# Query preparation for the next block moved from the end of an attention block to its head boundaries

## The reference

```python
xn = x / jnp.maximum(l2, 1e-12) * scale_norm * gamma
qkv = jnp.einsum('bnc,fc->bnf', xn, w_qkv)
q = q * scale_attn
sim = jnp.einsum('bihd,bjhd->bhij', q, k)
sim = jnp.where(causal_mask, neg, sim)
attn = jax.nn.softmax(sim, axis=-1)
out = jnp.einsum('bhij,bjhd->bihd', attn, v)
return jnp.einsum('bnf,cf->bnc', out, w_out)

x = x + _layernorm(_L0_attn_ref(_layernorm(x, axis=-1), ...), axis=-1)
x = x + _layernorm(_L0_ffn_ref(_layernorm(x, axis=-1), ...), axis=-1)
```

## Time and profile before

| what | us |
|---|---|
| time, median of 2 runs (7944.98 and 7990.62) | 7967.8 |
| profiled execution, its own time | 7980.3 |
| its span, slowest core (core 2) | 7978.8 |
| spans of the 8 cores | 7902.2 to 7978.8 |
| TensorE busy, share of the span | 4850.2, 61% |
| ScalarE busy | 3005.3, 38% |
| VectorE busy | 2903.3, 36% |
| GpSimd busy | 481.4, 6% |

### The profile page before, as it was taken

How to read it: one execution, slowest core, us unless ns; L and a number is a source line. 1 busy time by engine, 2 the same in 40 slices (tenths; PEclk the granted TensorE clock), 3 DMA queues, 4 the chain that set the end, 5 groups by cost and what they waited for, 6 DMA issues and landing times.

```text
span 7978.8 us, 56275 instructions; the slowest of 8 cores (7902.2 to 7978.8 us)
## 1 busy us (share of the span) xinstructions
PE 4850.2 (61%) x18281; PEld 1766.1 (22%) x18624; DVE 2903.3 (36%) x4937; ACT 3005.3 (38%) x4569; POOL 481.4 (6%) x612
## 2 busy tenths in 40 slices
PE   3545666877875233366566676887814767766553
PEld 1221222222221111122122222222202222222211
DVE  4444333122123666444333322222124333334445
ACT  1212444564563121122234554464612333333332
POOL 0000100000000000000000000000021011010000
PEclk8776888988987666566688888798956778878776
DMA  2111111001001122200211101001043011010111
GB/s 76 36 64 45 48 41 41 24 27 37 22 24 49 60 90 77 95 32 27 71 48 43 42 27 39 22 27 36 12 128 104 0 37 48 3 44 25 42 43 61
DMA packets 120312, 362.13 MB, mean 45 GB/s; under 512 B 24464, under 2 KB 24464, under 8 KB 120016
## 3 DMA queue, kind: packets, MB, share of 16 engines
q1 hardware_dynamic: 120016, 358.51, 13.5%
HBM read 291.07 MB, written 67.37 MB: 45 GB/s over the span
## 4 chain that ended last, share of the span: by engine, by line
PE 51%; DVE 22%; DMA 12%; ACT 8%; issue 3%; POOL 2%; SPq 1%; DVEq 0%; ACTq 0%
PE pf L1119 9%; PE pf L805 8%; PE pf L845 8%; PE pf L834 7%; ACT probs L815 4%; PE pf L638 3%; PE pf L898 3%; PE pf L664 3%; DMA xq<-xbuf 3%; PE pf L739 3%; PE pb L481 2%; DMA xbuf<-xq 2%; POOL probs L823 2%; DVE xq L571 2%; PE pf L1123 2%
## 5 line engine op out<-in xcount | busy, mean ns | idle before, releaser
L815 ACT ACTIVATE probs<-pf,negM_col 128x512 bf16<-128x512 f32 x2304 | 1585.4, 688 | 819.7 <-PE pf L805 764.4
L834 PE MATMUL pf<-probs,v_sb 128*128 128x512 bf16 x2286 | 908.9, 398 | 461.5 <-ACT probs L815 267.1
L481 PE MATMUL pb<-ident_bf,prep_bf 128*128 128x128 bf16 x1536 | 198.6, 311 | 1356.9 <-DVE prep_bf L337 461.0
L856 DVE RECIPROCAL rcp_row<-pf 1x512 f32<-1x512 f32 x128 | 428.3, 3346 | 1449.1 <-PE pf L845 1445.3
L845 PE MATMUL pf<-probs,ones_col 128*1 128x512 bf16 x2304 | 893.8, 388 | 8.1 <-ACT probs L815 3.7
L805 PE MATMUL pf<-qT,kT 128*128 128x512 bf16 x2178 | 855.4, 401 | 4.0 <-issue 4.0
L823 POOL TENSOR_SCALAR_AFFINE_SELECT probs<-probs 128x512 bf16<-128x512 bf16 x512 | 314.4, 614 | 5457.1 <-ACT probs L815 5457.1
L1131 ACT ACTIVATE ySB<-pf,bcol 128x512 bf16<-128x512 f32 x384 | 264.0, 687 | 730.7 <-PE pf L1123 727.2
L540 ACT ACTIVATE sq<-pb 128x1024 bf16<-128x1024 bf16 x128 | 131.1, 1024 | 907.0 <-DVE cols L534 907.0
L481 PEld LDWEIGHTS pb<-ident_bf,prep_bf 128*128 128x128 bf16 x1536 | 148.0, 141 | 1412.5 <-DVE prep_bf L337 422.2
L1119 PE MATMUL pf<-hT,wbuf 128*128 128x512 bf16 x1497 | 402.9, 414 | 48.7 <-ACT ySB L1131 41.7
(11 more groups left out here) (134 smaller groups left out, 5531.9 us busy)
## 6 DMA issues: line engine op xcount, KB each, us to landing
xq<-xbuf SPq DMA_DIRECT2D x128, 512.0 KB, 3.2
xbuf<-xq SPq DMA_DIRECT2D x96, 512.0 KB, 2.6
xq<-x SPq DMA_DIRECT2D x64, 512.0 KB, 3.5
rcp_bc<-rowrt SPq DMA_DIRECT2D x128, 256.0 KB, 3.1
xq4f<-xbuf SPq DMA_DIRECT2D x64, 512.0 KB, 4.0
wstage<-wqkvT SPq DMA_DIRECT2D x48, 512.0 KB, 4.4
wstage_i<-qwT SPq DMA_DIRECT2D x48, 512.0 KB, 3.7
screp<-scT SPq DMA_DIRECT2D x384, 64.0 KB, 2.3
```

Source lines behind the costliest of these rows:

```text
L481: v = p.add("tensor", lambda e, j=j: e.transpose(M.pb[pslot][:, j, :], M.prep_bf[:, prep_slot, j * 128:(j + 1) * 128], M.ident_bf[:]), wai ...
L815: ev = p.add("scalar", lambda e, kc=kc, h=h, ps=ps: e.activation(M.probs[:, kc % 2, :], ps[:], AF.Exp, bias=M.negM_col[:, h:h + 1], scale= ...
L834: p.add("tensor", lambda e, h=h, kc=kc, pO=pO: e.matmul(pO[:], M.v_sb[:, kc, h * 128:(h + 1) * 128], M.probs[:, kc % 2, :], start=(kc == 0 ...
L856: rc = p.add("vector", lambda e, pR=pR: e.reciprocal(M.rcp_row[:], pR[0:1, :]), waits=rw, inc="ve")
```

## The change

The four tiles of `q_prep` are written one by one behind heads 0, 1, 2 and 3 of the block before, each behind that head's normalisation. Nothing is written behind head 4. The groups of `q_mm` for heads 0, 1 and 2 are written behind heads 5, 6 and 7. The other five groups stay behind the output projection. The last block (qt = 7) has no next block and is as before, and so is the preparation of block 0 ahead of the loop. No operation is added or removed.

```diff
-    def q_prep(qt):
-        evs = []
-        for tt in range(4):
+    def q_prep_tile(qt, tt, evs):
+        for tt in (tt,):
...
+    def q_prep(qt):
+        evs = []
+        for tt in range(4):
+            q_prep_tile(qt, tt, evs)
         return ("ve", max(evs))
+
+    def q_mm_group(fo, xnT_ready):
+        pfk = M.pf[fo % 2]
...
+        return qev
...
             p.pO_gate[hp] = ("ve", nv)
+            if qt + 1 < nq:
+                if h == 0:
+                    qp_evs = []
+                if h < 4:
+                    q_prep_tile(qt + 1, h, qp_evs)
+                    if h == 3:
+                        xnT_ready = ("ve", max(qp_evs))
+                else:
+                    qev_n = q_mm_group(h - 5, xnT_ready) if h >= 5 else None
+        attnout_ready = ("ve", p.c("ve"))
         p.feat8_gate = None
-        attnout_ready = ("ve", p.c("ve"))
-
-        if qt + 1 < nq:
-            xnT_ready = q_prep(qt + 1)
...
         if qt + 1 < nq:
-            qT_ready = q_mm(qt + 1, xnT_ready)
+            for fo in range(3, H):
+                qev_n = q_mm_group(fo, xnT_ready)
+            p.xnT_free[0] = p.add("scalar", _nop, inc="nf0")
+            qT_ready = ("ae", qev_n)
             negM_evs = bound_prep(qt + 1, qT_ready)
```

More of the change, by code:

```diff
@@ L729, in q_prep @@
             evs.append(emit_prep_to_xnT(p, M, tt, 0, tp))
+    def q_prep(qt):
+        evs = []
+        for tt in range(4):
+            q_prep_tile(qt, tt, evs)
         return ("ve", max(evs))
+    def q_mm_group(fo, xnT_ready):
+        pfk = M.pf[fo % 2]
+        w0 = [xnT_ready, wq_ready]
+        if p.pf_gate[fo % 2]:
+            w0.append(p.pf_gate[fo % 2])
+        for fi in range(NF):
+            mv = p.add("tensor", lambda e, fo=fo, fi=fi, pfk=pfk: e.matmul(
+                pfk[:], M.wbuf1[:, fi, fo * 128:(fo + 1) * 128],
+                M.xnT[:, 0, fi, :], start=(fi == 0), stop=(fi == NF - 1)),
+                waits=(w0 if fi == 0 else ()),
+                inc=("mm" if fi == NF - 1 else None))
+        qev = p.add("scalar", lambda e, fo=fo, pfk=pfk: e.activation(
+            M.qT[:, fo, :], pfk[:], AF.Copy), waits=[("mm", mv)], inc="ae")
+        p.pf_gate[fo % 2] = ("ae", qev)
+        return qev
     def q_mm(qt, xnT_ready):
         for fo in range(H):
[L734 to L746, removed]
+            qev = q_mm_group(fo, xnT_ready)
         p.xnT_free[0] = p.add("scalar", _nop, inc="nf0")
```

## The result

| what | before | after |
|---|---|---|
| median of all runs, us | 7958.2 (10 runs) | 8519.6 (11 runs) |
| lowest and highest | 7867.1 to 7990.6 | 8432.1 to 8620.1 |
| profiled execution, its span | 7978.8 (core 2) | 8477.3 (core 3), its own time 8478.8 |

The changed kernel takes 1.0733 times as long (95% interval 1.0668 to 1.0798), 561 us more in the medians. In some executions of either kernel one die (cores 0 to 3 or 4 to 7) is slowed by a few per cent; all ratios here leave these out and so differ a little from the quotient of the medians. Forecast were 8590 us, +621, within 8430 to 8700.

A forecast was written before the change was run, and what follows sets the result against it. In the attention blocks neither TensorE nor ScalarE is full, so TensorE's queue order and waits matter. Twelve blocks at 46.1 us (553) plus 68 for both blocks 0 gave +621 on 7967.8: 8590 us, range 8430 to 8700.

The forecast's parts named there:

- The stall: Behind heads 0 to 3 of blocks 1 to 6, transposes waiting for the apply hold the next head's scores: 12.1 us each.
- The end of the block: Last row sum to last projection evacuation, blocks 1 to 6: the preparation leaves it, as in block 7, -10.3 us.
- The groups: Query groups moved behind heads 5, 6 and 7 of blocks 1 to 6: +0.4 us a block in sum.
- The clock: TensorE restarts at low clock behind each stall in blocks 1 to 6: 1.9 us a stalled head, bounds 0 and 2.3.
- The step that failed: Taking the clock cost of a stalled head, 1.9 us, from head 0's extra 1.8 and 2.15 us over head 1.
- Block 0: In each layer's block 0, with four-step heads, stalls partly replace waits: +34 us, both +68, lower bound 46.
- The sum: Whole kernel: 553 us for twelve blocks plus 68 for both blocks 0, +621 us, forecast 8590 us.
- The stages that were not touched: Part A, both feed-forward stages and block 7 should keep their times; moves by tens of microseconds would mean wrong.
- The hidden load: Rival: at all 56 stalls the apply waits for the multiply alone, -78 us, 8512 us; chance 0.09.
- free: Rival: transposes wake TensorE's clock before the next head in blocks 1 to 6, -91 us, 8499 us; chance 0.09.
- low throughout: Rival: TensorE's clock stays low through heads 1 to 4 of blocks 1 to 6, +358 us, 8948 us; chance 0.08.
- ready matmuls pass waiting ones: Rival: on TensorE the transposes do not hold the next head, -90 us in all, 7880 us; chance 0.03.

The follow-up runs named there:

- wait-only run: Kernel before plus an empty TensorE step behind heads 0 to 3 of blocks 0 to 6 that waits for the head's multiply: 8498.8 us, ratio 1.0727.
- the last two versions: The changed order reworked, with four or six query groups behind head 7 (pipelined, six groups): 7725.5 and 7686.5 us.
- tiles-only profile: Changed kernel with the tiles behind heads 0 to 3 but all eight query groups behind the projection: 8524.9 us, ratio 1.0761 to the kernel before.
- keeping TensorE busy: Changed kernel with 44 matmuls of unused result on TensorE ahead of each tile's transposes: 8465.7 us, the median of two runs 103 us apart.
- apply first: Changed kernel with each tile's load and apply written ahead of the head's reciprocal, transposes left in place: 7830.7 us, ratio 0.9858 to the kernel before.
- pipelined: Changed kernel with apply right behind the reciprocal, transposes one head later, four query groups behind head 7: 7725.5 us, ratio 0.9751 to the kernel before.
- six groups: As pipelined, with six query groups behind head 7 instead of four: 7686.5 us, ratio 0.9703 to the kernel before.
- issued early: Changed kernel with each tile's load written ahead of the head's first DMA, apply still behind the multiply: 8443.8 us, ratio 1.0658 to the kernel before.
- A pause of 4.2 us: Kernel before plus an empty TensorE step behind heads 0 to 3 of blocks 0 to 6 that waits for the head's reciprocal: 8253.2 us, ratio 1.0418.

## Why the prediction was right

**The stall.** Forecast were 12.1 us for each of four heads. The pauses grew by 47.45 us a block, 11.9 a head. The wait-only run shows that waiting for the multiply makes 9.0 of them. Its parts at one boundary: 4.73 us from the row sum to the broadcast (forecast 4.67), 5.00 from there to the apply (5.3), 1.70 on to the score matmul (2.1), and the 0.07. The load landed last, as forecast, but by 0.61 us only. The rest of its price is that the multiply itself began 3.69 us behind the broadcast DMA instead of 3.09, with the load in flight beside it.

**The end of the block.** Forecast -10.3, measured 26.57 - 37.83 = -11.3. Block 7 was the right model, since the wait for the multiply was what came late next. It costs TensorE its clock in turn, and filling it is what the last two versions gain there.

**The groups.** Forecast were +4.7 behind the heads and -4.3 in the query stretch; the tables give +4.9 and -4.0, and the tiles-only profile about 1 us a block in sum (forecast 0.4).

**The clock.** This is the largest term off: 1.9 us forecast for a stalled head, (78.01 - 72.81) / 4 = 1.3 measured (1.1 to 1.2 between the same cores of the other die, 4 to 7). Over 48 heads that is 29 us too much. The step that failed took the price from head 0 of two blocks. Over all twelve blocks of the kernel before, head 0 has 5.4 us at 0.50 and takes 1.7 us more than a head of 1 to 4; behind a stall of the change 4.1 us of the head lie at 0.50 and it takes 1.3 us more; with the wait for the multiply alone it is 5.1 and 1.6. In all three a head loses about 0.32 us for each microsecond at the low level, so the change's heads were cheaper because the level came back sooner. That the clock makes the 1.3 us was shown by keeping TensorE busy.

**Block 0.** Forecast +34, measured +29.1. The estimate for a head at low clock was 8.0 us from its score matmul on. These heads take 27.94 / 4 = 7.0 from the first exponential, and their score matmul starts 0.7 us ahead of it, which makes 7.7. The distance of the stalled heads was forecast as 20.1 us. Reciprocals of heads 1 and 4 of block 0 after, from VectorE's timeline:

```profile
666.07 3.35 DVE L864 RECIPROCAL rcp_row<-pf 1x512 f32<-1x512 f32 x1 [7.04 <-PE pf L853]
...
724.64 3.35 DVE L864 RECIPROCAL rcp_row<-pf 1x512 f32<-1x512 f32 x1 [7.04 <-PE pf L853]
```

They are 58.57 us apart, 19.5 a head. Up to the projection the two blocks 0 grew by 33.0 us in the mean, where 35 and 3 for the groups were forecast, and behind it they gave back 3.9 (4.3).

**The sum.** 12 x 42.8 + 2 x 29.1 = 571 us against 621: the clock makes 29 of the difference, block 0 makes 10, the pauses and the end of the block 12 each. The groups and the rest of a block, 0.5 us a block each, go the other way. So the forecast is not right by large errors that cancel, but the core-by-core sums of 520 to 574 show it 47 to 101 us too high.

**The stages that were not touched.** I had written that I am wrong if they move by tens of microseconds, and they did. The spans of the two profiles differ by 498.5 us only, since the stretch between the layers' part B, and what follows the second, got shorter. Windows of the kernel before (core 2), then after (core 3):

```profile
2515.73:3908.72 1392.99, 575.01 (x2528) 269.55 (x2570) 743.58 (x1548) 260.79 (x471) 0.00 (x0) 0.63 0.20 68
5799.20:7978.80 2179.60, 1200.12 (x4681) 447.29 (x4768) 876.75 (x1348) 704.69 (x1022) 166.84 (x96) 0.72 0.15 49
```

```profile
2796.18:4141.57 1345.39, 537.88 (x2570) 260.11 (x2570) 743.65 (x1548) 260.72 (x470) 0.00 (x0) 0.65 0.20 70
6331.32:8477.25 2145.93, 1172.85 (x4768) 440.58 (x4768) 872.89 (x1348) 704.51 (x1022) 168.22 (x96) 0.74 0.16 50
```

In the attention blocks core 3 took 577 us more than core 2 before (571, and 6 in the two blocks 7); with 2 us ahead of them and these 47.6 and 33.7 us less it comes to the 498.5. VectorE's and ScalarE's busy times hardly differ in the two stretches and TensorE's are longer before. What goes with the 47.6 and 33.7 us is a granted clock of 0.81 for long stretches. Before, core 2 had 321 us at that level in the first stretch and 464 in the second; after, core 3 had 0 and 223, and 372 in layer 1's part B. These stretches fall on other cores and stages in each execution. They take part of the profiled pair's difference away, and they widen the distances between runs. Whether the idle time that the change adds makes them rarer is open; apply first and pipelined had none on any core in their profiles, six groups 393 us on core 1.

**The rivals.** The hidden load comes out as the size of one small term: issued early it brings 571 - 12 x 38.3 - 2 x 27.0 = 57 us less, of the 78 that this rival gave it, and part of that is variation between executions. The clock is neither free nor low throughout. That ready matmuls pass waiting ones is excluded: at all 56 boundaries the score matmul starts at least 11.3 us late, and in the wait-only run an empty step in front holds it in the same way.

## What to carry to other kernels

A piece of work that is moved ahead of a busy engine's next stage brings its whole chain of inputs with it. Follow that chain through every queue in the order of the code before moving it: here eight transposes, 0.5 us of work at full clock, stood behind an apply, the apply behind a multiply, and the multiply behind two DMAs, which made 12 us. The gain was to be had by putting the producer ahead of the long part of the chain (right behind the reciprocal), the consumer one head later, and ready matmuls into the wait that remains.

## What was not expected of the hardware

A pause of 4.2 us costs TensorE as much clock as one of 9.4. The extra time of a head behind it was 1.3 us for pauses of 12.2 us, 1.6 for 9.4 and 1.9 for 4.2, each a mean of 48 heads on the slowest core. The level of 0.81 told of below adds to some of them. On the cores on which it touched none of these heads, against the 72.6 us of heads 1 to 4 in apply first, it is 1.1 to 1.4 (cores 4 to 7), 1.5 to 1.6 (cores 0 to 3) and 1.6 to 1.7 us (cores 4 and 5). Of the long pause 9.8 us lie at 0.50 and 4.1 us of the head behind it; of the middle one 7.3 and 5.1; of the short one 2.0 and 5.3. What the short pause saves is low clock over idle time, which costs nothing. The long pause differs in kind too: about 1 us of it is the eight transposes, work that already runs at 0.50 ahead of the head. So shortening the wait to 4.2 us did not save its clock cost; it has to be filled, as with the 44 matmuls (0.1 us), or taken away, as in apply first and pipelined. The Trainium skill (Perfetto Trace Analysis, section Matmul Optimizations) asks for matmuls back to back in batches, and all these runs agree; none of them shows how short a pause would have to be to go free.

The level of 0.81 shows in one window on one core and not on another: in the kernel after, the same 80 us of layer 1 on core 3 and core 6.

```profile
5515.00:5595.00 80.00, 74.56 (x226) 20.11 (x224) 11.90 (x6) 49.40 (x73) 6.12 (x10) 0.81 0.04 10
```

```profile
5515.00:5595.00 80.00, 71.75 (x241) 21.36 (x240) 12.11 (x6) 52.84 (x77) 9.52 (x16) 1.00 0.03 10
```

Core 3 gets through 73 exponentials there and core 6 through 77. In each profile that has the level, two neighbouring cores (0 and 1, 2 and 3, and so on) have it at nearly the same times, in episodes of up to about 120 us, which other pairs need not share: here cores 2 and 3 have it and the other six do not. What sets it off is open.
